# Moving the row passes of two layer norms and an eviction to ScalarE, with one mask product for two heads, in a fused attention and FP4 feed-forward block

## What is computed

```python
mod = (silu(c) @ wmod).reshape(16, 6, 1, 256)      # sa, ca, ga, sb, cb, gb per batch
h = layernorm(x) * (1 + ca) + sa
x = x + ga * attention(h)      # 16 heads of 16, ALiBi slopes, causal, softmax; then @ o_w.T + o_b
h = layernorm(x) * (1 + cb) + sb
x = x + gb * ffn(h)
# attention: Q = h@q_w.T+q_b, K likewise, V = h@v_w.T+v_b; softmax(QK/4 + slope*rel, causal) @ V
# ffn: fp4(silu(fp4(h)@gate.T) * (fp4(h)@up.T)) @ down.T, fp4 = blocks of 16, scale = max|x|/6,
#      rounded to the grid 0, .5, 1, 1.5, 2, 3, 4, 6 and multiplied back
```

## Time and profile before

| | |
|---|---|
| median of 3 runs | 4124.66 us (4122.55 to 4128.27) |
| profiled execution | 4125.13 us, its span 4123.1 us |
| busy, share of the span | PE 89%, DVE 77%, ACT 46%, PEld 47%, POOL 31% |
| granted TensorE clock, mean | 0.956 of 2.4 GHz |

### The profile page before, as it was taken

The page is one execution under the profiler, slowest core; times in us unless marked ns, Lnnn a source line. Parts: engine busy times, 40 slices in busy tenths (PEclk is TensorE's granted clock), DMA queues, the critical chain, the costliest instruction groups (busy, mean ns, idle before and its releaser), DMA issues.

```text
span 4123.1 us, 57870 instructions
## 1 busy us (share of the span) xinstructions
PE 3656.7 (89%) x21300; PEld 1920.1 (47%) x21300; DVE 3191.6 (77%) x6061; ACT 1916.1 (46%) x3471; POOL 1289.3 (31%) x918
## 2 busy tenths in 40 slices
PE   4899989999888989988899899998988999899966
PEld 2344444544444444454544445444454544445435
DVE  9877877787787778878787777877778788776835
ACT  2454544445444544545455454444545455454531
POOL 5214233242332424224142332423224132331223
PEclk7899999999999999999999999999999999999987
DMA  7141322323232331323323332331313313322010
GB/s 130 27 87 28 63 45 50 58 45 60 43 55 40 63 54 31 63 39 56 58 36 54 51 53 49 54 57 37 63 32 63 58 31 59 50 48 44 22 26 11
DMA packets 158188, 205.51 MB, mean 50 GB/s; under 512 B 44036, under 2 KB 98004, under 8 KB 157908
## 3 DMA queue, kind: packets, MB, share of 16 engines
q1 hardware_dynamic: 157908, 201.82, 28.8%
HBM read 63.78 MB, written 17.89 MB: 20 GB/s over the span
## 4 chain that ended last, share of the span: by engine, by line
PE 52%; DVE 27%; DMA 6%; issue 5%; ACT 4%; POOL 4%; SPq 3%; DVEq 0%; POOLq 0%; ACTq 0%
PE banks L681 8%; PE banks L814 8%; PE banks L704 7%; PE banks L664 7%; PE banks L798 6%; DVE banks L1094 5%; PE banks L791 5%; ACT arena L865 3%; DMA xa<-in_x 3%; PE banks L760 3%; PE banks L807 2%; SPq L552 2%; DMA sums<-oT 2%; PE banks L772 2%; PE banks L729 2%
## 5 line engine op out<-in xcount | busy, mean ns | idle before, releaser
L865 ACT ACTIVATE arena<-banks 128x512 f32<-128x512 f32 (+1 forms) x2432 | 1291.4, 582 | 1175.8 <-PE banks L667 748.5
L1094 DVE CUSTOM_DVE_ANT_0 banks<-banks,mask 128x640 f32<-128x640 f32 (+3 forms) x1024 | 1032.6, 1042 | 65.3 <-PE banks L704 58.1
L664 PE MATMUL banks<-qa,ka 105*128 105x512 bf16 (+3 forms) x3072 | 833.9, 332 | 95.7 <-ACT arena L865 70.8
L704 PE MATMUL banks<-ka,qa 102*128 102x512 bf16 (+3 forms) x3072 | 762.8, 335 | 124.7 <-DVE top L1094 87.4
L681 PE MATMUL banks<-arena,va 128*17 128x512 f32 (+3 forms) x6144 | 648.9, 497 | 20.5 <-ACT arena L865 16.4
L664 PEld LDWEIGHTS banks<-qa,ka 105*128 105x128 bf16 x3072 | 281.0, 98 | 657.0 <-ACT arena L865 370.9
L704 PEld LDWEIGHTS banks<-ka,qa 102*128 102x128 bf16 x3072 | 258.7, 99 | 466.6 <-DVE top L1094 162.1
L999 POOL TENSOR_TENSOR hid<-hid,tm 128x704 f32<-128x704 f32 x128 | 217.3, 1698 | 714.2 <-DVE hid L1068 714.2
L1092 DVE TENSOR_REDUCE top<-banks 128x2 f32<-128x768 f32 (+3 forms) x384 | 381.2, 1039 | 57.0 <-PE banks L709 55.4
L814 PE MATMUL banks<-wdT,hqT 128*128 128x256 f32 x1536 | 371.4, 393 | 2.9 <-ACT hqT L908 2.8
L791 PE MATMUL banks<-wguT,xqT 128*128 128x352 f32 x1024 | 333.7, 472 | 0.7 <-ACT xqT L899 0.7
(11 more groups left out here) (146 smaller groups left out, 4894.1 us busy)
## 6 DMA issues: line engine op xcount, KB each, us to landing
qa<-parts SPq DMA_DIRECT2D x384, 128.0 KB, 4.5
ka<-parts SPq DMA_DIRECT2D x384, 128.0 KB, 5.2
xa<-in_x SPq DMA_DIRECT2D x16, 1024.0 KB, 10.0
rsumT<-rsum_dram SPq DMA_DIRECT2D x64, 256.0 KB
onT<-oT SPq DMA_DIRECT2D x256, 64.0 KB, 4.3
xr<-in_x SPq DMA_DIRECT2D x64, 256.0 KB, 2.7
out_x<-xr SPq DMA_DIRECT2D x64, 256.0 KB, 6.3
ffn_rows<-rows_dram SPq DMA_DIRECT2D x16, 384.0 KB, 7.7
```

The source lines that it names most:

```text
L664: mm = pe.matmul(ps[:, m * w:(m + 1) * w], ka[g][0:KT, h, kt * P:(kt + 1) * P], qa[g][0:KT, h, q0:q0 + w], start=heads < G, stop=heads == ...
L704: mm = pe.matmul(ps[:, at:at + z - a], qa[g][0:KS, h0 + m, qt * P:(qt + 1) * P], ka[g][0:KS, h0 + m, a:z], start=qt > 0, stop=qt == 0 or h ...
L865: nc.scalar.activation(probs[:, s % P_SLOTS, j * heads:(j + 1) * heads, 0:w], ps[:, 0:heads * w].rearrange("p (h q) -> p h q", h=heads), A ...
L1094: nc.vector.tensor_tensor_reduce(out=ps, in0=ps, in1=mask[:, S - w:S], scale=1.0, scalar=MASKED, op0=ALU.add, op1=ALU.max, accum_out=tops) ...
```

## The change

- `N3` moves to ScalarE: Identity with scale rs and bias ms = -mean * rs, from a new last step of the root (L1035 ff.); the wait is on `row_scales`. Batch 0 keeps the old form.
- `LN` becomes `LX` on ScalarE (two 128x256 Identity passes with rs and ms) and two VectorE instructions of 128x512 (times cb, plus sb), in place of four of 128x256.
- `V` leaves through ring A: one ScalarE copy of 128x1024 a half, without the bias. As softmax rows sum to one, the value bias is a constant after the output projection: two new jobs, once in the kernel, `BB` (DVE) and `BO` (PE, then DVE), add v_b @ o_w.T to `bo_row`.
- The triangle product is made once for two heads of a bank, in `T` for tiles of two heads of 256 columns (4 products a step become 2) and in `S` for the second query tile (4 become 2).
- Costs and lags in `plan()` are rewritten, and so the order of all streams. The largest: XA's lag 7 to 12, MUL gets a lag of 8 (was 0.06), S on DVE 0.05 to 0.1 less, SM 1.5 to 0.9, SPL 6.5 to 7, HQ on POOL 3.4 to 3.15.

```diff
-            p.add("SP", ("XA", b), 0.7, at, ("POOL", ("SPL", b - 1, 3)), lag=7.0)
+            p.add("SP", ("XA", b), 0.7, at, ("POOL", ("SPL", b - 1, 3)), lag=12.0)
-                p.add("DVE", ("N3", b, h), 1.75, at + 0.07 * L + h, ("DVE", ("N2", b)), ("DVE", ("N3", b, 0)) if h else None)
+                p.add("ACT", ("N3", b, h), 1.6, at + 0.07 * L + h, ("DVE", ("N2", b)), ("ACT", ("N3", b, 0)) if h else None)
-               ("ACT", ("T", b - 1, NG - 1, NS - 1, jobs_of(NS - 1) - 1)), ("PE", ("V", b, 0)) if v else None, ring="D", on="DVE",
-               takes_cost=1.75, banks=2, then=(("PE", ("PV", b - 1, NG - 1, NS - 1)),))
+               ("ACT", ("T", b - 1, NG - 1, NS - 1, jobs_of(NS - 1) - 1)), ("PE", ("V", b, 0)) if v else None, ring="A", on="ACT",
+               takes_cost=1.05, banks=2, then=(("PE", ("PV", b - 1, NG - 1, NS - 1)),))
-            p.add("POOL", ("MUL", b, g // 2), 2.4, due + 10.0, *((("SP", (k, b, n)) for n in (g - 1, g) for k in ("NUM", "RBC"))))
+            p.add("POOL", ("MUL", b, g // 2), 2.4, due + 10.0, *((("SP", (k, b, n)) for n in (g - 1, g) for k in ("NUM", "RBC"))), lag=8.0)
-            p.add("DVE", ("LN", b, r), 2.6, due, ("DVE", ("LR", b)), ("ACT", ("WT", 0, GU // 2)), ("ACT", ("WD", 0, C - 1, 1)), ("SP", ("FROW", b)), ("PE", ("XT", *pair(-2))),
+            p.add("ACT", ("LX", b, r), 0.8, due - 2, ("DVE", ("LR", b)), ("ACT", ("WT", 0, GU // 2)), ("ACT", ("WD", 0, C - 1, 1)), ("PE", ("XT", *pair(-2))),
                   ("DVE", ("HQ", *tile(2 * r - 3))))
+            p.add("DVE", ("LN", b, r), 1.4, due, ("ACT", ("LX", b, r)), ("SP", ("FROW", b)))
...
                         for m in range(heads):
                             h = j * heads + m
                             mm = pe.matmul(ps[:, m * w:(m + 1) * w], ka[g][0:KT, h, kt * P:(kt + 1) * P], qa[g][0:KT, h, q0:q0 + w],
-                                           start=heads < G, stop=heads == G or s not in DIAGONAL, skip_group_check=True)
-                            if s in DIAGONAL and heads < G:
-                                mm = pe.matmul(ps[:, m * w:m * w + P], identb[:, :], maskT[:, :], start=False, stop=True,
-                                               skip_group_check=True)
+                                           start=heads < G and m == 0, stop=heads == G or s not in DIAGONAL, skip_group_check=True)
+                        if s in DIAGONAL and heads < G:
+                            mm = pe.matmul(ps[:, 0:heads * w].rearrange("p (h q) -> p h q", h=heads)[:, :, 0:P], identb[:, :],
+                                           maskT[:, :].unsqueeze(1).broadcast_to((P, heads, P)), start=False, stop=True,
+                                           skip_group_check=True)
...
+                    if kind == "N3":
+                        act.wait_ge(row_scales[0], b + 1)
+                        for t in range(4 * e[2], 4 * e[2] + 4):
+                            ins = nc.scalar.activation(xa[:, t, :], xa[:, t, :], ACT.Identity, bias=ms[0][:, t:t + 1],
+                                                       scale=rs[0][:, t:t + 1])
+                        ins.then_inc(xn_ready, 1)
+                        continue
+                    if kind == "LX":
+                        r = e[2]
+                        act.wait_ge(row_scales[1], b + 1)
+                        if b or r >= 2:
+                            act.wait_ge(a_full, in_a["XT", b, r - 2] if r >= 2 else in_a["XT", b - 1, r + 2])
+                        for j in range(2):
+                            t = 2 * r + j
+                            ins = nc.scalar.activation(xb[r % 2][:, j * D:(j + 1) * D], xr[:, t, :], ACT.Identity,
+                                                       bias=ms[1][:, t:t + 1], scale=rs[1][:, t:t + 1])
+                        ins.then_inc(rows_scaled, 1)
+                        continue
...
+                    if kind == "V":
+                        t = 4 * e[2]
+                        if b:
+                            act.wait_ge(pv_done, b * NG * NS)
+                        act.wait_ge(a_full, full)
+                        nc.scalar.copy(va[:, t:t + 4, :, 0:HD], ps.rearrange("p (t h w) -> p t h w", t=4, h=H)).then_inc(a_free, 1)
...
+                nc.vector.scalar_tensor_tensor(out=ms[k][:, :], in0=mv[k][:, :, 0], scalar=-1.0, in1=y,
+                                               op0=ALU.mult, op1=ALU.mult).then_inc(row_scales[k], 1)
...
+                    elif kind == "BB":
+                        dve.wait_ge(w_in[4], 16 * 4)
+                        nc.vector.tensor_copy(delta[0][:, :].rearrange("p (c n) -> p c n", c=C),
+                                              bvc[:, :].unsqueeze(2).broadcast_to((P, C, P))).then_inc(bv_ready, 1)
+                    elif kind == "BO":
                         dve.wait_ge(d_full, in_d[e])
...
+                        dve.wait_ge(rows_scaled, b * NPAIR + r + 1)
+                        step(nc.vector.tensor_tensor(h2, h2, cb_row.unsqueeze(1).broadcast_to((P, 2, D)), ALU.mult))
+                        step(nc.vector.tensor_tensor(h2, h2, sb_row.unsqueeze(1).broadcast_to((P, 2, D)), ALU.add))
```

More of the change, by code:

```diff
@@ L265, in attention @@
                 p.add("PE", ("PV", b, g, s), 1.9e-3 * w + 0.03, due + 3, ("ACT", ("T", b, g, s, jobs_of(s) - 1)),
-                      ("PE", ("PV", b, g, s - 1)) if s else None, ("DVE", ("V", b, 1)) if (g, s) == (0, 0) else None, lag=0.22,
+                      ("PE", ("PV", b, g, s - 1)) if s else None, ("ACT", ("V", b, 1)) if (g, s) == (0, 0) else None, lag=0.22,
                       banks=1 if s in FIRST else 0, holder=("ACT", ("CO", b, g, c)) if s in FIRST else None)
@@ L296, in weights @@
                    ring="A", on="ACT", takes_cost=0.6)
+        p.add("DVE", ("BB", 0), 0.4, 30.0)
+        pe(("BO", 0), 0.95, 40.0, ("DVE", ("BB", 0)), ring="D", on="DVE", takes_cost=0.45)
         for g in range(NG):
@@ L315, in feed_forward @@
             pe(("O", b, r), 1.75, at + 2.0 + r, ("POOL", ("MUL", b, 0)), ("POOL", ("MUL", b, 1)), ("POOL", ("WG", b)),
-               ring="D", on="DVE", takes_cost=2.0, then=(("POOL", ("FOLD", b, r)), ("DVE", ("LN", b - 1, NPAIR - 1))))
-        p.add("DVE", ("LR", b), 2.4, at + 6.0, *(("DVE", ("O", b, r)) for r in range(NPAIR)))
+               ring="D", on="DVE", takes_cost=1.76, then=(("POOL", ("FOLD", b, r)), ("DVE", ("LN", b - 1, NPAIR - 1))))
+        p.add("DVE", ("LR", b), 2.5, at + 6.0, *(("DVE", ("O", b, r)) for r in range(NPAIR)))
         first, every = at + 0.06 * L, 0.235 * L
@@ L337, in feed_forward @@
                 pe(("UP", b, t), 2.4, late + 2, ("PE", ("GA", b, t, 1)), ("PE", ("UP", *tile(t - 1))), ring="D", on="DVE",
[L338 to L341, removed]
+                   takes_cost=0.89, banks=2, then=(("ACT", ("GA", b, t, 1)),))
+                p.add("DVE", ("HR", b, t), 1.6, late + 4, ("DVE", ("UP", b, t)), ("DVE", ("HQ", *tile(t - 1))))
+                p.add("DVE", ("HQ", b, t), 2.95, late + 6, ("DVE", ("HR", b, t)), ring="Q")
+                p.add("POOL", ("HQ", b, t), 3.15, late + 8, ("DVE", ("HQ", b, t)), takes="Q")
                 for k in range(2):
@@ L420, in adaln_block @@
         stats = sb("stats", [P, T, 6])
-        mv, rs = ([sb(f"{n}{k}", shape) for k in range(2)] for n, shape in (("mv", [P, T, 2]), ("rs", [P, T])))
+        mv, rs, ms = ([sb(f"{n}{k}", shape) for k in range(2)] for n, shape in (("mv", [P, T, 2]), ("rs", [P, T]), ("ms", [P, T])))
         ve, tn = sb("ve", [P, T]), sb("tn", [P, T])
@@ L699, in run @@
                                       start=True, stop=False, skip_group_check=True)
+                        paired = 2 if qt == 1 else 1
                         for m in range(heads):
@@ L761, in run @@
                                                wvT[:, c, :], start=(c == 0), stop=(c == C - 1))
+                        mm.then_inc(a_full, 1)
+                    elif kind == "BO":
+                        ps = open_banks(e)
+                        pe.wait_ge(bv_ready, 1)
+                        for c in range(C):
+                            mm = pe.matmul(ps[:, 0:D], delta[0][:, c * P:(c + 1) * P], woT[:, c, :], start=(c == 0), stop=(c == C - 1))
                         mm.then_inc(d_full, 1)
```

82 lines of the change are left out of this document (29 added, 53 removed).

## The result

The changed kernel takes 4085.62 us (median of 4 runs, 4083.98 to 4095.55) against 4123.6 for the kernel before on the same chips: a ratio of 0.9914, 95% interval 0.9893 to 0.9934. It is faster by 0.9%, 38 us, where 160 were forecast. The profiled execution is the slowest of the four; its span is 4092.6 us, 30.5 less than before.

A forecast was written before the change was run, and what follows sets the result against it. The prediction took PE and the holes in its stream to bound the kernel. From 4125 us it subtracted 105 + 42 + 25 - 14 = 158, giving 3967, rounded to 3965 us; the range was 3875 to 4105.

The forecast's parts named there:

- MUL's lag: PE's wait at output projection O: a lag of 8 fills it, 0 to 8.2 us a batch, 7.0 taken, 105 us.
- XA's lag: VectorE's wait for xa, with PE starving later: longer lag wins 3.0 us in each of 14 batches, 42 us.
- the other costs: Planner costs SM, SPL, HQ, S: only shift order, -2 to +2 us a batch, 0 taken.
- moved work, mask products: N3, LN and V partly moved off VectorE, +25 and -14 us; shared triangle products, 0.
- VectorE's relief: V, N3 and part of LN leave VectorE: PE waits less for it, 1.8 us a batch, 25 us won.
- ScalarE's price: exp queues behind the new N3, LX and V on ScalarE: 1.0 us a batch taken, -14 us.
- The mask products: One triangle product for two heads has the same columns: 0 counted, at most 0.5 us a batch.
- (b): Rival: the hole at O moves, PE stands behind GA or DN; 4072 us; 0.20, including what lies towards the forecast.
- (c): Rival: ScalarE becomes the place of the wait, exp stands behind 7 new waits, slower; 4188 us; chance 0.10.

The follow-up runs named there:

- e2: The kernel before with one edit, MUL's lag 0.06 to 8: 3996.6 us, ratio 0.9692.
- e7: The kernel before with both lags of the change, MUL 8 and XA 12, and nothing else: 4021.3 us, ratio 0.9751.
- e3: The kernel before with all rewritten costs and lags for the jobs both have, none of the other edits: 4109.9 us, ratio 0.9964.
- e13: e10 with XA's lag at 7 again in place of 12: 3910.9 us, ratio 0.948.
- e10: The changed kernel with both GpSimd splits later (after XQ and after HQ) and SM's cost at 1.8 us: 3920.6 us, ratio 0.9511.
- e4: The changed kernel with the old costs and lags for the jobs both kernels have: 4119.9 us, ratio 0.9984.
- e5: e4 with MUL's lag of 8: 3989.9 us, ratio 0.9675.
- e11: The kernel before with every cost, lag and list rule of e10 for the jobs both have: 4033.6 us, ratio 0.9777.
- e12: e10 with a triangle product for each head again, costs and lists unchanged: 3909.2 us, ratio 0.948.
- e1: The changed kernel with each batch's first split placed after quantisation XQ(b-2, 0) in GpSimd's list: 4031.4 us, ratio 0.9773.
- e6: e1 with each batch's second split also placed after quantisation HQ(b-2, 1) in GpSimd's list: 3970.1 us, ratio 0.9629.
- e8: e1 with SM's cost at 1.8 us in place of 0.9: 3975.5 us, ratio 0.964.
- e15: The changed kernel with MUL's lag at 0.06 again, all else kept: 4153.3 us, ratio 1.0061.

## Why the prediction was right or wrong

The time lay inside the range, but the forecast of 160 us was four times the 38 measured, and the time lay in the range partly by luck: errors of both signs met. Three measured kernels lie between the kernel before and the changed one, each with one more part of the change (in another order the parts might weigh otherwise):

| part | forecast, us won | measured, us won |
|---|---|---|
| MUL's lag (before to e2) | 105 | 127 to 130 |
| XA's lag (e2 to e7) | 42 | -25 |
| the other costs (e7 to e3) | 0 | -89 |
| moved work, mask products (e3 to the change) | 11 | 24 |

By its steps:

- **MUL's lag**: 105 us forecast, 127 to 130 measured alone (e2), 8.5 to 8.6 us for each of 15 batches, just above the upper end of 8.2. The reading of the hole was right; O's wait is at 19 us as said.
- **XA's lag**: +42 forecast, wrong in sign: -25 (e7) and -10 (e13, at the edge of the noise; with that lag at 7 VectorE waits only 6.6 us for xa in e10's lists). I took a wait of VectorE that came before a hole of PE for its cause. e7 removes the wait and gains nothing.
- **VectorE's relief and ScalarE's price**: +25 and -14, 11 us net. Measured as a whole: 4 to 7 us with the old costs (e4, e5), 24 with the new ones, 113 with the costs and rules of e10 (e10, e11; with the lists different too). So 11 was of the right size for the lists at hand. VectorE is busy 187.7 us a period where 183 was forecast: the root steps took 115 us in the kernel in place of 48, which is 4.2 us a batch. I also took the mean durations of V and N3, 3.3 and 3.2 us a batch, while the busy times of their groups, 45.3 and 43.8 us in 16 batches, give 2.8 and 2.7, as instructions in a row overlap (128 times 0.406 us is 52, not 43.8). The sizes of the operations were good:

These groups of the changed kernel (busy us, mean ns, idle before) answer to the earlier trace rows:

```profile
L1205 DVE TENSOR_TENSOR xb<-xb,ffn_rows 128x512 f32<-128x512 f32 x64 | 72.7, 1136 | 2.2
L1204 DVE TENSOR_TENSOR xb<-xb,ffn_rows 128x512 f32<-128x512 f32 x64 | 52.0, 812 | 4.6 <-ACT xb L880 3.4
...
L880 ACT ACTIVATE xb<-xr,ms,rs 128x256 f32<-128x256 f32 x128 | 69.4, 593 | 96.5 <-DVE ms L1073 96.5
L869 ACT ACTIVATE xa<-xa,ms,rs 128x256 f32<-128x256 f32 x120 | 62.2, 597 | 37.2 <-DVE ms L1073 37.2
...
L891 ACT COPY va<-banks 128x1024 f32<-128x1024 f32 x32 | 32.3, 1014 | 83.9 <-PE banks L767 83.9
```

  N3 and LX take 0.59 to 0.60 us for 256 columns (0.57 estimated), V's copy 1.01 (1.02), the table loads stay at 61 and 61, and LN takes 1.95 us instead of 3.6 (2.6 estimated). PE waits 23.8 us for exp at this place, less than the 70.8 before: the blocks on ScalarE show no cost there.
- **The mask products**: 0 forecast; 0 to -11 us (e12).
- **The other costs (SM, SPL, HQ, S), which "only shift order", at -2 to +2 us a batch, 0 taken**: with XA's lag this is the step that failed. From e7 to e3 they cost 89 us, 6 us a period: PE's wait for L1210 (56.2 us) and most of that at MT (4.4 to 30.3) come with them, and the split moves from LN onto the roots. In the changed kernel the order costs 54 us at the first split beside the roots (e1), 61 us at the second beside HQ (e6) and 56 us with SM at 0.9 against 1.8 (e8, a whole new order), 171 us in all, of which e10 gives back 165. The first of the three needs MUL's lag too, as e15 shows. I had seen both halves: the long two-input instructions and that SM takes longer with GpSimd running. But I priced the collision only where it already stood, in LN, and counted the roots at their undisturbed time. I did not ask what the new order puts beside them.

The rule of the Trainium skill (SBUF — State Buffer, "Who interferes with whom") that I weighed for LN alone, that a VectorE instruction with two SBUF inputs and a GpSimd instruction that reads SBUF wait for each other in whole, is what these rows show for the roots: steps of 166 ns that end with a GpSimd instruction of 2.12 us. By it every list has to be read in pairs, VectorE beside GpSimd; a cost for each job alone, as the planner has it, cannot express it. The sum went on as if it did.

Of the rivals, (b), that the hole at O moves, came nearest in number, 4072 beside 4086, but by luck: its sum has nothing for O's hole and 42 us for XA, while O's hole was worth 127 to 130 us (e2) and XA's lag cost some. Nor did PE stand behind GA or DN through a shorter stretch of the feed-forward; it stood for VectorE steps stretched by GpSimd, DN's eviction among what they delayed. (c) did not come about: ScalarE waits for the roots 96.5 us at LX and 37.2 us at N3, but exp behind it has slack.

## What to carry to other kernels

A lag or cost that the trace contradicts at one hole is worth an experiment of its own before it is bundled: here one number was worth 3.1%, and the package around it took most of that back. Where two engines block each other, read the lists side by side after any change of order; a hair of timing decided whether they met, so secure the order by what one engine waits for. Relief of an engine that is not the bound can look worthless while the order makes holes (7 us between e2 and e5, 113 between e11 and e10, where the lists differ too). After an edit to a planner's costs, count what else moved: e1 changed one engine's list alone and so shows its cause, e8 changed all of them. And a wait that stands just before a hole need not be its cause.

## What the runs showed of the hardware

Two things that the rows show. A 128x8 step of VectorE, 166 ns alone, took up to 1985 ns beside a GpSimd instruction of 2.1 us (the changed kernel, 96 instances, none over 170 ns in e1). And the single-input steps of HQ were stretched as well: 0.53 us became 2.33 beside GpSimd's split.
